# A vision tower on one core: the five engines' programs in another order

## The reference

```python
h = patchify(x) @ W.T + b                        # 16 x 64 rows, 768 -> 256

v = h @ w1.T + b1                                # dynamic convolution: 16 heads, 31 taps
w = softmax((v @ ww.T + bw).reshape(..., 16, 31))
y = sum over k of w[..., k:k+1] * padded(v)[k:k+T]
a = layer_norm(h + y @ w2.T + b2) * gamma + beta
h = layer_norm(h + a)

gate = silu(act_quant(h) @ weight_quant(w_gate).T)   # act_quant: 127 / max|row|, round
up = act_quant(h) @ weight_quant(w_up).T             # weight_quant: -1, 0, 1 times a scale
f = act_quant(gate * up) @ weight_quant(w_down).T
out = layer_norm(h + f)
```

## Time and profile before

| | us |
|---|---|
| median of 3 runs | 127.07 (126.97 to 127.29) |
| span of the profiled execution | 125.7 |
| busy: TensorE | 107.9 |
| busy: VectorE | 86.1 |
| busy: GpSimd | 80.8 |
| busy: ScalarE | 66.1 |

### The profile page before, as it was taken

The page is one execution under the profiler, slowest core; times in us unless marked ns, Lnnn a source line. Parts: engine busy times, 40 slices in busy tenths (PEclk is TensorE's granted clock), DMA queues, the critical chain, the costliest instruction groups (busy, mean ns, idle before and its releaser), DMA issues.

```text
span 125.7 us, 2379 instructions
## 1 busy us (share of the span) xinstructions
PE 107.9 (86%) x718; PEld 67.8 (54%) x718; DVE 86.1 (69%) x202; ACT 66.1 (53%) x109; POOL 80.8 (64%) x153
## 2 busy tenths in 40 slices
PE   6997999999999999999999999999998653884400
PEld 2673465866856486467555576668573322453200
DVE  5014593644965768799998999888696676898410
ACT  0042128639527444594633988766783836575200
POOL 6994000059700865867974868798888888888870
PEclk9999999999999999999999999999999999689975
DMA  3899999962321122232313112212300100011112
GB/s 104 260 357 340 399 420 422 400 255 21 63 24 17 42 25 23 53 51 42 32 42 30 14 42 25 22 42 27 64 0 0 42 0 0 4 46 42 44 43 82
DMA packets 23467, 12.45 MB, mean 99 GB/s; under 512 B 18141, under 2 KB 21981, under 8 KB 23070
## 3 DMA queue, kind: packets, MB, share of 16 engines
q1 hardware_dynamic: 21936, 10.46, 29.4%
q10 hardware_dynamic: 1518, 1.84, 4.8%
HBM read 9.95 MB, written 2.34 MB: 98 GB/s over the span
## 4 chain that ended last, share of the span: by engine, by line
PE 63%; POOL 19%; issue 5%; DMA 4%; ACTq 2%; DVE 2%; POOLq 1%
PE bank L339 12%; PE bank L417 11%; PE bank L400 11%; PE bank L383 6%; PE bank L444 5%; POOL q L1080 5%; DMA bias_cols<-in_cols 4%; PE bank L472 4%; PE bank L488 3%; POOL rstd L999 3%; POOL f L1087 3%; PE bank L357 3%; ACTq L676 2%; POOL res L1055 2%; POOL veps L998 2%
## 5 line engine op out<-in xcount | busy, mean ns | idle before, releaser
L339 PE MATMUL bank<-xT,tokW 128*128 128x256 f32 x72 | 16.7, 381 | 0.0
L417 PE MATMUL bank<-conv_w,vpad 128*32 128x128 f32 x256 | 15.8, 398 | 0.0
L1043 POOL TENSOR_TENSOR taps<-probs,inv_total 128x256 f32<-128x256 f32 x8 | 5.1, 634 | 15.7 <-DVE inv_total L741 15.4
L339 PEld LDWEIGHTS bank<-xT,tokW 128*128 128x128 f32 x72 | 13.5, 190 | 2.6 <-issue 0.9
L400 PE MATMUL bank<-wl,h1T 128*128 128x496 f32 x32 | 14.6, 578 | 0.0
L641 ACT ACTIVATE gu<-bank,sc 128x512 f32<-128x512 f32 x16 | 11.0, 686 | 5.3 <-PE bank L472 5.1
L527 PE MATMUL bank<-w_q,q2T 128*128 128x256 f16 x64 | 8.5, 273 | 3.9 <-ACT q2T L655 3.5
L812 DVE TENSOR_TENSOR gu<-gu,bank 128x512 f32<-128x512 f32 x16 | 10.8, 681 | 1.3 <-ACT gu L641 0.6
L998 POOL TENSOR_SCALAR veps<-mv 128x1 f32<-128x1 f32 x16 | 3.6, 225 | 11.9 <-DVE mv L751 10.9
L417 PEld LDWEIGHTS bank<-conv_w,vpad 128*32 128x32 f32 x256 | 8.3, 122 | 5.2 <-issue 1.4
L1080 POOL TENSOR_SCALAR q<-gu,sc 128x512 f16<-128x512 f32 x14 | 10.0, 716 | 1.4 <-DVE sc L829 0.2
(11 more groups left out here) (119 smaller groups left out, 237.2 us busy)
## 6 DMA issues: line engine op xcount, KB each, us to landing
xT<-in_xT SPq DMA_DIRECT2D x3, 768.0 KB, 16.9
w_raw<-in_wg SPq DMA_DIRECT2D x1, 1024.0 KB, 13.2
w_raw<-in_wu SPq DMA_DIRECT2D x1, 1024.0 KB, 15.2
w_raw<-in_wd SPq DMA_DIRECT2D x1, 1024.0 KB, 16.9
shear<-taps SPq DMA_DIRECT2D x8, 128.0 KB, 1.8
conv_w<-shear SPq DMA_DIRECT2D x64, 16.0 KB, 2.0
out_dram<-res SPq DMA_DIRECT2D x8, 128.0 KB
tokW<-in_tokW SPq DMA_DIRECT2D x6, 128.0 KB, 5.0
```

Of the source, the lines that this page charges most:

```text
L339: last = nc.tensor.matmul(ps_embed(pair, m), tokW[:, k, m * P:(m + 1) * P], xT[:, pair, k, :], start=(k == 0), stop=(k == KC_PATCH - 1))
L417: last = nc.tensor.matmul(ps_yT[j * SLOT:(j + 1) * SLOT, k, :], vpad[:, s, h, :], conv_w[:, s, :, h], start=(par == 0), stop=(par == 1))
```

## The change

Each engine's list of calls is written in another order. No call is added or taken away, and functions, buffers and semaphores are the same. One piece of TensorE's list, one of SyncE's:

```diff
-            residual(3); up(1, 1); gate(1, 1); conv(3); logits(6); in_transposes(2); project_out(3); gate(2, 0)
-            up(2, 0); values(4); up(2, 1); gate(2, 1); logits(7); inner_transposes(0, 0); inner_transposes(0, 1)
-            residual(4); conv(4); down(0, 0); down(0, 1); project_out(4); in_transposes(3); values(5)
+            residual(3); logits(6); project_out(3); up(1, 0); gate(1, 1); inner_transposes(0, 0); up(1, 1)
+            inner_transposes(0, 1); in_transposes(2); values(4); gate(2, 0); residual(4); down(0, 0); down(0, 1)
+            gate(2, 1); logits(7); conv(4); up(2, 0); inner_transposes(1, 0); project_out(4); up(2, 1)
...
-            put_taps(4); spread(4); put_taps(5); spread(5); put_taps(6); spread(6); put_taps(7); spread(7)
-            store(0); store(1); store(2); store(3); store(4); store(5); store(6); store(7)
+            put_taps(4); spread(4); put_taps(5); spread(5); put_taps(6); spread(6); store(0); put_taps(7)
+            spread(7); store(1); store(2); store(3); store(4); store(5); store(6); store(7)
```

More of the change, by code:

```diff
@@ new lines, in _ @@
+            in_transposes(3); values(5); gate(3, 0); residual(5); inner_transposes(1, 1); conv(5); up(3, 0)
+            project_out(5); values(6); down(1, 0); down(1, 1); residual(6); gate(3, 1); up(3, 1); conv(6)
+            values(7); inner_transposes(2, 0); inner_transposes(2, 1); in_transposes(4); project_out(6)
+            gate(4, 0); up(4, 0); conv(7); gate(4, 1); inner_transposes(3, 0); up(4, 1); in_transposes(5)
+            down(2, 0); residual(7); down(2, 1); project_out(7); inner_transposes(3, 1); up(5, 0); gate(5, 0)
@@ new lines, in _ @@
+            out_h1(0); exps(0); out_h1T(1, 1); weight_sum(2); exps(1); weight_round(1); exps(2); exps(3)
+            out_h1T(2, 0); out_yT(0); out_h1T(2, 1); out_v(1); out_yT(1); out_h1(1); exps(4); centre(0)
+            out_v(2); quant_in(0); out_h1(2); out_q1T(0); weight_finish(1); centre(1); exps(5); out_h1T(3, 0)
+            out_yT(2); nc.scalar.preload_act_table(ACT.Silu); silus(0, 0); quant_in(1); out_q1T(1); silus(0, 1)
+            out_v(3); centre(2); out_h1T(3, 1); out_yT(3); silus(1, 0); out_h1(3); quant_in(2); silus(1, 1)
@@ L957, in _ @@
-            top_logits(4); shift(4); attn_norm(0); mid_stats(0); mid_variance(0); weight_scales(2, 3)
-            mid_absmax(0); attn_stats(1); attn_variance(1); mid_scales(0); out_scales(0); attn_centre(1)
-            attn_norm(1); mid_stats(1); mid_variance(1); tap_sums(4); tap_inverses(4); top_logits(5); shift(5)
-            mid_absmax(1); mid_scales(1); out_scales(1); tap_sums(5); tap_inverses(5); attn_stats(2)
-            attn_variance(2); attn_centre(2); inner(0, 0); attn_norm(2); mid_stats(2); mid_variance(2)
@@ L962, in _ @@
-            inner(0, 1); mid_absmax(2); inner_absmax(0); mid_scales(2); out_scales(2); inner(1, 0)
-            inner_scales(0); down_scale(0); inner(1, 1); inner_absmax(1); inner_scales(1); down_scale(1)
-            top_logits(6); shift(6); attn_stats(3); attn_variance(3); inner(2, 0); attn_centre(3); attn_norm(3)
-            mid_stats(3); mid_variance(3); inner(2, 1); top_logits(7); tap_sums(6); tap_inverses(6)
-            mid_absmax(3); shift(7); mid_scales(3); out_scales(3); inner_absmax(2); attn_stats(4)
@@ new lines, in _ @@
+            top_logits(4); shift(4); attn_norm(0); mid_stats(0); tap_inverses(3); mid_variance(0); mid_absmax(0)
+            attn_stats(1); attn_variance(1); mid_scales(0); attn_centre(1); out_scales(0); top_logits(5)
+            tap_sums(4); tap_inverses(4); attn_norm(1); mid_stats(1); mid_variance(1); shift(5); mid_absmax(1)
+            tap_sums(5); mid_scales(1); inner(0, 0); attn_stats(2); attn_variance(2); attn_centre(2)
+            tap_inverses(5); inner(0, 1); attn_norm(2); mid_stats(2); mid_variance(2); out_scales(1)
@@ new lines, in _ @@
+            inner_absmax(0); mid_absmax(2); inner_scales(0); top_logits(6); mid_scales(2); attn_stats(3)
+            shift(6); attn_variance(3); down_scale(0); attn_centre(3); out_scales(2); attn_norm(3); mid_stats(3)
+            mid_variance(3); inner(1, 0); inner(1, 1); inner_absmax(1); inner_scales(1); mid_absmax(3)
+            out_stats(0); top_logits(7); out_variance(0); mid_scales(3); tap_sums(6); shift(7); tap_inverses(6)
+            down_scale(1); inner(2, 0); attn_stats(4); attn_variance(4); attn_centre(4); inner(2, 1)
@@ new lines, in _ @@
+            attn_norm(4); mid_stats(4); out_scales(3); mid_variance(4); tap_sums(7); inner_absmax(2)
+            tap_inverses(7); inner_scales(2); mid_absmax(4); attn_stats(5); attn_variance(5); mid_scales(4)
+            attn_centre(5); out_scales(4); inner(3, 0); attn_norm(5); mid_stats(5); inner(3, 1); mid_variance(5)
+            inner_absmax(3); inner_scales(3); out_stats(1); down_scale(2); mid_absmax(5); mid_scales(5)
+            out_variance(1); out_scales(5); attn_stats(6); attn_variance(6); attn_centre(6); inner(4, 0)
@@ new lines, in _ @@
+            add_beta(4); quant_inner(1, 0); quant_inner(1, 1); inv_std_out(0); inner_limit(3); normalise(6)
+            scale_h3(3); inv_std_attn(4); result(0); add_beta(5); inv_std_mid(4); normalise(7)
+            quant_inner(2, 0); quant_inner(2, 1); inv_std_attn(5); inner_limit(4); add_h3(1); add_beta(6)
+            scale_h3(4); inv_std_mid(5); quant_inner(3, 0); quant_inner(3, 1); inv_std_out(1); inv_std_attn(6)
+            result(1); inner_limit(5); inv_std_mid(6); add_beta(7); add_h3(2); quant_inner(4, 0)
```

99 lines of the change are left out of this document (40 added, 59 removed).

## The result

The changed kernel is a little faster: 126.31 us at the median of 20 runs (124.90 to 128.23) beside 126.88 of the kernel before in the same sessions (20 runs, 126.56 to 127.55). The ratio is 0.9930 (0.9908 to 0.9952). Ratios leave out runs that lie over 1.5% above the fastest of their kernel, here seven of the changed kernel and none of the kernel before; medians hold all runs, and their ratio is 0.9955. Twelve more runs in another session (after_again) give 0.9973 (0.9937 to 1.0008), which alone can't be told from no change.

The account below looks back on a forecast made before the run. TensorE's list was taken to bound the first two thirds, POOL's the last. 125.7 - 2.6 + 2.65 + 0.9 + 0.2 = 126.85, plus 1.37 from span to median, gave 128.2 us, slower by 0.9%; range 125.2 to 130.5.

Parts of the forecast that it names:

- What bounds the kernel: TensorE's list sets the end of the first two thirds, up to 90.8 us; POOL's list that of the last.
- The first 53 us: nothing: Start of the kernel: TensorE does the same operations by 53.3 us instead of 53.12; nothing charged.
- The hole on POOL: minus 2.6: POOL's idle stretch from 33.83 to 40.88 us takes in normalise(2) and weight_round(2), putting POOL 2.6 us ahead at 74 us.
- What eats the lead: plus 2.65: Behind 74 us: POOL's waits come to 4.1 us against 1.45 now, 2.65 more, so POOL ends near 122.2.
- Waits (1) and (2): POOL waits for late tap inverses from VectorE: 0.7 us before normalise(6), 0.8 us before normalise(7).
- (3): POOL's short waits for tiles 4 and 5 (attention's variance, h1b, quantiser scales): together 0.9 us.
- (4): At quant_inner(5): mid_scales(6) stands behind tile 7's attention norm, so POOL waits 0.45 us for tile 5's scale.
- (5): At inv_std_out(3): POOL waits 0.85 us behind VectorE's delay from tile 7's attention norm.
- TensorE late, and handing over: plus 0.9: From conv(6) on: TensorE 2.3 us late, 0.3 of tile 7's delay reaching the end; waits for operands add 0.6.
- rival C: TensorE's clock falls at tile 7's four gate pairs, adding 2.1 us: 130.3 us, slower still; chance 0.14.
- The end: plus 0.2: Last stores: result(6) behind inv_std_out(7), stores leave in tile order, so store(7) goes at 122.9 instead of 122.7.
- The rule weighed: VectorE and GpSimd shut each other out of SBUF; moving the third weight's passes could save 1.1 us, not taken.

Follow-up runs that it names:

- a_round2: Changed kernel with weight_round(2) moved on GpSimd out of the early hole to directly ahead of weight_clip(2): 127.19 us, ratio 0.9993 to the kernel before.
- b_hole: Kernel before with only normalise(2) and weight_round(2) moved ahead of inv_std_attn(0), the third weight's mean and scales moved to suit: 127.17 us, ratio 1.0001.
- after_look1: Changed kernel unedited, one more profiled execution: 125.78 us.
- after_look2: Changed kernel unedited, another profiled execution: 128.69 us.
- b_full: Kernel before with the hole filled, all third-weight passes ahead of tile 2's statistics and quant_inner(1) ahead of tile 3's: 126.29 us, ratio 0.9977.

## Why the prediction was wrong

*What bounds the kernel* was right. In all 19 profiles the span ends 3.5 to 4.2 us behind POOL's last operation, whatever the order, and a_round2, whose length is 0.83 us above the changed kernel's, is 0.9 above it in time. One reading was off: the earlier trace rows shows the clock below 9 in four of the last six slices, not in all six.

*The first 53 us: nothing* held: the first tap weights come 11.42 us behind the bias row, before 11.44, and conv(2), which ends the set of operations named there, ends at 54.04, or 53.0 without the late start; the walk had 53.3, before it was 53.12.

*The hole on POOL: minus 2.6* was right as a sum, by luck, and not in its parts. POOL's waits up to 74 us, without the one before normalise(6), fell by 15.73 - 13.85 = 1.88, and add_beta(0), which the term does not hold, gives 0.70: 2.58. But a lead is not a gain by itself, as b_hole shows; weight_round(2) in the hole is worth 0.8, not 1.98.

*What eats the lead: plus 2.65* is the step that failed. It measured 0.71: from 72.4 on POOL waits 2.16 us in the changed kernel against 1.45 before, where I had 4.1. Waits (1) and (2) are not there: the inverse of tile 6 ends at 75.86 and POOL takes it at 75.95, that of tile 7 ends at 81.82, taken at 82.03. Of (3) 0.59 is left; (4) is not there; (5) is 0.32 instead of 0.85.

The walk ran too slow, and more so on VectorE than on POOL. Without the late start the two inverses end at 74.9 and 80.8, where I had 76.2 and 82.7, and mid_scales(6) starts at 100.6 instead of 102.45: 1.3 to 1.9 early. POOL was free for the two at 74.8 and 80.9, where I had 75.6 and 81.9: 0.8 to 1.0 early. Two reasons can be seen. The walk put each instruction behind the full duration of the one ahead, but on VectorE and ScalarE the next one, where it doesn't need that one's result, starts some 0.1 us before that has passed. The changed kernel on VectorE:

```profile
66.49 0.43 DVE L746 BATCH_NORM_STATS2 stats<-bank 128x6 f32<-128x256 f32 x1
66.84 0.66 DVE L727 TENSOR_TENSOR probs<-bank,top 128x496 f32<-128x496 f32 x1
```

0.35 us lie between the starts, not 0.43. Over dozens of instructions this puts VectorE late against a POOL whose gaps I had counted; how much of the 1.3 to 1.9 it makes was not separated. The other reason is in wait (1) itself. I charged 0.66 for shift(7) ahead of the inverse, but from the table load's start to the inverse's end pass 3.35 us (72.51 to 75.86), before 3.24 (70.11 to 73.35), only 0.11 more: tap_sums(6) starts 0.03 behind the end of exps(6), where before it stood 0.38 behind it, after top_logits(7). A decision on 0.7 us hung on all this; I had said that it was less than the walk's error and then forecast by it.

The largest wait, 0.98 before add_beta(7), I had not seen at all: store(0) holds SyncE for 0.76 us and the eight issues of spread(6) took 5.07 instead of 4.43, so tile 7's weights come late for conv(7).

*TensorE late, and handing over: plus 0.9.* conv(6) ends at 87.84, 1.8 us later than before if the late start is taken off; residual(6) and down(1), now ahead of it, are 1.09 of that, so TensorE is 0.7 late where I had 2.3. In the profiled execution it costs nothing: tile 7's gates start 0.1 later than before and end at 111.83, before at 111.38, so 0.55 earlier without the late start, because the clock held. It costs in others, by rival C's mechanism. Its price of 2.1 us set 1.06 from a timeline against 0.54 from a chain; a timeline has 0.59 for a pair at full clock, and 4 x 0.47 is 1.9. Measured is 1.96 in the one profile where tile 6's and tile 7's gates lost the clock. How many executions that is the means don't tell exactly; 8 of 32 have 0.967 or less. I had given C to all executions or none. The Trainium skill (TensorE: Matmul & The Clock Gate, "What's actually happening") says that the watch on TensorE's activity runs freely and is not reset by a kernel's start; after_look1 and after_look2, one program with a granted clock of 1.00 and of 0.51 over the same gates, agree with it but don't show it.

*The end: plus 0.2* was too small. The last store is issued at 122.0, 0.72 behind POOL's end, before 0.51 behind it, as forecast; but the span ends 4.0 behind POOL's end, before 3.5, so the term measured 0.5. Why 0.3 more pass behind the last issue no run shows.

*The rule weighed.* VectorE's attn_norm is nowhere held by a weight pass in the new order, its mean fell from 634 to 493 ns:

```profile
L768 DVE SCALAR_TENSOR_TENSOR a<-a,rstd,h1b 128x256 f32<-128x256 f32 x8 | 3.9, 493 | 0.7 <-POOL rstd L999 0.4
```

Against my reading, those 1.1 us may not have been free: in b_full, where the pass is moved away too and line 768 takes 0.48 us there, normalise(6) comes at 72.68 instead of 73.43, 0.4 earlier if the earlier start of that execution (24.98 instead of 25.35) is taken off. How much of this, and of b_full's 0.46 us, is due to the pass was not separated.

The size follows. The sum with the terms as measured is 125.7 - 2.58 + 0.71 + 0.5 = 124.33; the changed kernel's span without its late start is 124.3, so nothing is left for the 0.9 of TensorE. Around a span lie 1.8 us (127.06 - 125.3), not 1.37: the profiled execution before was some 0.4 above the median that I set it against. That gives 126.1 for an execution that starts in time and keeps its clock. The median of all 20 runs is 126.31; late rows and low clocks are in it, and their shares were not separated.

## What to carry to other kernels

A lead on the engine that ends last is worth only what work it finds ready in its next waits: follow it to the next operand that another engine sets, and reorder so that finished tiles' work stands there. When a forecast hangs on who is first by less than the error of the walk, forecast both. And look at the granted clock in several executions: the same program can keep it in one and lose it in the next, and an order that has removed the slack can pay for it.
